# Turning the later contexts and x by 64 rows on both row halves, into the free columns of V's two PSUM banks

## The reference

```python
h = layernorm(x, gamma, beta)                 # x: (8, 256, 256)
Q = (h @ Wq).reshape(B, NQ, 16, 64)           # Wq: 256 x 1024
K = (context @ Wk).reshape(B, NC, 16, 64)     # context: (8, 256, 192)
V = (context @ Wv).reshape(B, NC, 16, 64)
attn = softmax(einsum('bihd,bjhd->bhij', Q, K)) * 64 ** -0.5
vals = einsum('bhij,bjhd->bihd', attn, V).reshape(B, NQ, 1024)
out = x + vals @ Wo + bo
```

## Time and profile before

| What | Value |
|---|---|
| time, median of three runs | 329.81 us |
| time of the profiled execution | 330.24 us |
| its span | 328.2 us |
| PE busy | 320.4 us, 98% of the span |
| DVE busy | 253.5 us, 77% |
| ACT busy | 253.6 us, 77% |
| POOL busy | 155.8 us, 47% |
| mean granted TensorE clock | 0.999 |

### The profile page before, as it was taken

How to read it: one execution, slowest core, us unless ns; L and a number is a source line. 1 busy time by engine, 2 the same in 40 slices (tenths; PEclk the granted TensorE clock), 3 DMA queues, 4 the chain that set the end, 5 groups by cost and what they waited for, 6 DMA issues and landing times.

```text
span 328.2 us, 9691 instructions
## 1 busy us (share of the span) xinstructions
PE 320.4 (98%) x3771; PEld 281.6 (86%) x3771; DVE 253.5 (77%) x591; ACT 253.6 (77%) x798; POOL 155.8 (47%) x288
## 2 busy tenths in 40 slices
PE   5999999999999999999999999999999999999995
PEld 3978888899888889988889988889988888988874
DVE  5798887877778787786878778787777878668784
ACT  4899897877778877888777878787777887776862
POOL 5586578625644256433563336731564425233330
PEclk9999999999999999999999999999999999999999
DMA  6980000020001100020000200002000000000000
GB/s 180 256 257 8 0 2 3 2 91 2 0 3 41 51 3 0 2 90 2 3 3 1 90 2 2 2 1 91 2 2 2 32 3 2 2 3 32 2 3 32
DMA packets 10860, 10.70 MB, mean 33 GB/s; under 512 B 960, under 2 KB 10304, under 8 KB 10816
## 3 DMA queue, kind: packets, MB, share of 16 engines
q1 hardware_dynamic: 10336, 9.77, 10.2%
q10 hardware_dynamic: 416, 0.33, 0.3%
q0 software_dynamic: 64, 0.00, 0.0%
HBM read 8.00 MB, written 2.10 MB: 31 GB/s over the span
## 4 chain that ended last, share of the span: by engine, by line
PE 92%; DVE 3%; ACT 2%; DMA 1%; issue 0%; DVEq 0%
PE mix_ps L919 17%; PE ring_ps L890 14%; PE ring_ps L985 13%; PE o_ps L1025 12%; PE ring_ps L943 11%; PE ring_ps L1062 9%; PE ring_ps L1102 8%; PE ring_ps L1109 3%; ACT prob L469 2%; DMA c_in<-in_ctx_dram 1%; PE ring_ps L963 1%; PE mix_ps L861 1%; PE mix_ps L853 1%; DVE prob_t L830 1%; DVE qk_lo L722 1%; PE mix_ps L1089 0%
## 5 line engine op out<-in xcount | busy, mean ns | idle before, releaser
L378 POOL TENSOR_SCALAR prob<-prob,inv 128x256 f32<-128x256 f32 x192 | 90.3, 487 | 106.5 <-DVE inv L693 106.4
L469 ACT ACTIVATE prob<-ring_ps,neg_max 128x256 f32<-128x256 f32 x256 | 118.4, 476 | 21.6 <-DVE neg_max L686 21.5
L686 DVE TENSOR_REDUCE neg_max<-ring_ps 128x2 f32<-128x512 f32 x128 | 81.4, 678 | 0.4 <-PE ring_ps L890 0.3
L919 PE MATMUL mix_ps<-prob_t,v_sb 128*64 128x256 f32 x496 | 60.6, 386 | 0.3 <-DVE prob_t L830 0.3
L722 DVE TENSOR_TENSOR qk_lo<-ring_ps,qk_hi 128x512 fp32r<-128x512 f32 x64 | 44.2, 691 | 18.2 <-ACT qk_hi L481 18.1
L830 DVE COPY prob_t<-ring_ps 128x512 f32<-128x512 f32 x64 | 41.2, 686 | 21.0 <-PE ring_ps L1062 21.0
L469 ACT ACTIVATION_READ_ACCUMULATOR prob<-ring_ps,neg_max 128x1 f32 x256 | 53.2, 208 | 0.0
L481 ACT ACTIVATE qk_hi<-ring_ps 128x512 fp32r<-128x512 f32 x64 | 38.7, 605 | 13.9 <-PE ring_ps L985 13.9
L919 PEld LDWEIGHTS mix_ps<-prob_t,v_sb 128*64 128x64 f32 x496 | 32.8, 136 | 17.9 <-issue 0.4
L890 PE MATMUL ring_ps<-qk_hi 64*128 64x256 f32 x256 | 39.6, 302 | 0.1
L1062 PE MATMUL ring_ps<-ident,prob 64*128 64x64 f32 x1024 | 37.6, 222 | 0.2 <-DVE prob L712 0.2
(11 more groups left out here) (134 smaller groups left out, 687.4 us busy)
## 6 DMA issues: line engine op xcount, KB each, us to landing
x_in<-in_x_dram SPq DMA_DIRECT2D x8, 256.0 KB, 2.9
out_dram<-y_sb SPq DMA_DIRECT2D x7, 256.0 KB, 2.2
c_in<-in_ctx_dram SPq DMA_DIRECT2D x7, 192.0 KB, 2.9
w_raw<-in_L_xattn_Wq_dram SPq DMA_DIRECT2D x8, 128.0 KB, 3.3
w_raw<-in_L_xattn_Wo_dram SPq DMA_DIRECT2D x4, 256.0 KB, 4.2
w_raw<-in_L_xattn_Wk_dram SPq DMA_DIRECT2D x4, 128.0 KB, 4.1
w_raw<-in_L_xattn_Wk_dram SPq DMA_DIRECT2D x8, 64.0 KB, 3.7
w_raw<-in_L_xattn_Wv_dram SPq DMA_DIRECT2D x2, 256.0 KB, 4.8
```

The costliest lines, as they stand in the source:

```text
L378: last = nc.gpsimd.tensor_scalar(prob[:, e, r, :], prob[:, e, r, :], inv[:, e, r:r + 1], SCALE, ALU.mult, ALU.mult)
L469: last = nc.scalar.activation(prob[:, e, r, :], score_bank(u, e)[:, r * ROWS:(r + 1) * ROWS], ACT.Exp, bias=neg_max[:, e, r:r + 1], accum_ ...
L686: nc.vector.tensor_reduce(neg_max[:, e, :], score_bank(u, e)[:, :].rearrange("p (r j) -> p r j", r=RT), AX, ALU.max, negate=True).then_inc ...
L919: last = nc.tensor.matmul(ps[h * HALF:(h + 1) * HALF, first:first + ROWS], v_sb[:, w // RT % 2, j, p * P + h * HALF:p * P + (h + 1) * HALF ...
```

## The change

The sequences 0 and 1 keep their old transposes. For `b` of 2 to 7 TensorE does `turn_beside` in the same steps as before, but between `values(u + 1)` and `turn(u)`: eight transposes of 64 rows each, alternating between the upper and the lower row half of the array, the upper half's results going to columns 256 to 511 of V's first bank and the lower half's to those of V's second. VectorE copies these columns out to new SBUF tiles (`c_full`, `x_t`), the second bank while ScalarE copies V out of the first, then the first while ScalarE copies V out of the second. ScalarE now starts its copies of V only when `turn_beside` is done. The work that followed reads the SBUF tiles: `context_hi` and `hidden` on ScalarE come after the copies of the probabilities; the low part of the context moves one step later and is split, 128 rows on GpSimd (`context_lo_wide`) and 64 on VectorE (`context_lo_narrow`), followed by GpSimd's `context_for_values`; ScalarE's `context_again` moves two steps later.

```diff
         def context_bank(b):
-            return {0: ring[1][0], 1: o_ps}.get(b, mix_ps)
+            return (ring[1][0], o_ps)[b]
...
+            def context_lo_wide(b):
+                pool.wait_ge(c_hi_ready, b + 1)
+                nc.gpsimd.tensor_tensor(c_t[:, b % 2, 2, :], c_full[:, 0:ROWS],
+                                        c_t[:, b % 2, 0, :].bitcast(fp32), ALU.subtract)\
+                    .then_inc(c_lo_pool_ready, 1)
...
-                b = 1 if u == 2 else of_seq(u, TURN_C, 2)
+                b = 1 if u == 2 else of_seq(u, TURN_X, 2)
                 if b is not None:
+                    if b >= 2:
+                        context_lo_wide(b)
                     context_for_values(b)
...
                     if 2 <= u < STEPS - 1:
                         act.wait_ge(v_made, u + 2)
+                        it = beside(u)
+                        if it is not None:
+                            act.wait_ge(turned_beside, 2 * it[0] + 2)
                         for k, ps in enumerate(qk_banks(u + 1)):
+                            if it is not None and k == 1:
+                                act.wait_ge(beside_out, 2 * it[0] + 1)
                             last = nc.scalar.activation(
                                 v_sb[:, (u + 1) // RT % 2, (u + 1) % RT,
                                      k * V_HALF:(k + 1) * V_HALF],
                                 ps[:, 0:V_HALF], ACT.Copy)
+                            if it is not None and k == 0:
+                                last.then_inc(v_first, 1)
                         last.then_inc(v_ready, 1)
...
+                it = beside(u)
+                if it is not None:
+                    n, b, is_x = it
+                    act.wait_ge(beside_out, 2 * n + 2)
+                    if is_x:
+                        act.wait_ge(h_lo_ready, DT * b)
+                        hidden(b, x_t)
+                    else:
+                        context_hi(b, c_full)
...
+                b = of_seq(u, TURN_X, 2)
+                if b is not None:
+                    context_lo_narrow(b, c_full)
...
-                b = of_seq(u, TURN_C, 2)
-                if b is not None:
-                    context_lo(b, context_bank(b))
+                it = beside(u)
+                if it is not None:
+                    n, b, is_x = it
+                    if is_x:
+                        dve.wait_ge(h_full_ready, DT * b - 1)
+                    elif b >= 3:
+                        context_is_split(dve, b - 1)
+                    dve.wait_ge(turned_beside, 2 * n + 2)
+                    for half in (1, 0):
+                        if half == 0:
+                            dve.wait_ge(v_first, n + 1)
+                        out = (x_t if is_x else c_full)[:, :].rearrange("p (k x i) -> p k x i", x=2, i=HALF)
+                        nc.vector.tensor_copy(out[:, :, half, :],
+                                              qk_banks(u + 1)[half][:, V_HALF:2 * V_HALF]
+                                              .rearrange("p (k i) -> p k i", i=HALF))\
+                            .then_inc(beside_out, 1)
...
+            def turn_beside(u, n, b, is_x):
+                if is_x:
+                    pe.wait_ge(x_norm_ready, b + 1)
+                else:
+                    pe.wait_ge(c_loaded[b % 2], 16 * (b // 2 + 1))
+                for k, (d, r) in enumerate(itertools.product(range(DT), range(RT))):
+                    for half in range(2):
+                        own = slice(half * HALF, (half + 1) * HALF)
+                        if is_x:
+                            rows = x_norm[own, r, d * P:(d + 1) * P]
+                        else:
+                            first = d * (D_CTX - P)
+                            rows = c_in[own, b % 2, r, first:first + P]
+                        first = V_HALF + k * HALF
+                        last = nc.tensor.transpose(qk_banks(u + 1)[half][:, first:first + HALF],
+                                                   rows, ident[own, own])
+                        if k == DT * RT - 1:
+                            last.then_inc(turned_beside, 1)
...
             def scores(u):
                 if u >= 3:
                     pe.wait_ge(v_ready, u + 1)
+                    it = beside(u - 1)
+                    if it is not None:
+                        pe.wait_ge(beside_out, 2 * it[0] + 2)
...
-                b = of_seq(w, TURN_C, 2)
-                if b is not None:
-                    pe.wait_ge(c_lo_ready, b + 1)
-                b = of_seq(w, TURN_X, 1)
-                if b is not None:
-                    pe.wait_ge(h_full_ready, DT * b + 1)
+                if w == 1:
+                    pe.wait_ge(h_full_ready, DT + 1)
...
-                b = of_seq(u, TURN_C, 2)
-                if b is not None:
-                    pe.wait_ge(c_loaded[b % 2], 16 * (b // 2 + 1))
-                    turn_c(b, context_bank(b))
-                b = of_seq(u, TURN_X, 1)
-                if b is not None:
-                    pe.wait_ge(x_norm_ready, b + 1)
+                if u == 1:
+                    pe.wait_ge(x_norm_ready, 2)
                     turn_x((mix_ps, mix_ps), ROWS)
...
                 if 2 <= u < STEPS - 1:
                     values(u + 1)
+                it = beside(u)
+                if it is not None:
+                    turn_beside(u, *it)
                 if u == 0 or 2 <= u < STEPS:
                     turn(u)
```

More of the change, by code:

```diff
@@ L123, in cross_attention_block @@
         inv = sb("inv", [P, HEADS, RT])
+        c_full = sb("c_full", [P, 2 * ROWS])
+        x_t = sb("x_t", [P, DT * ROWS])
         ring = [(bank(f"ring{2 * k}_ps"), bank(f"ring{2 * k + 1}_ps")) for k in range(3)]
@@ L180, in cross_attention_block @@
         c_turned = sem("c_turned")
+        turned_beside = sem("turned_beside")
+        v_first = sem("v_first")
+        beside_out = sem("beside_out")
         h_full_ready = sem("h_full_ready")
@@ L187, in cross_attention_block @@
         c_lo_ready = sem("c_lo_ready")
+        c_lo_pool_ready = sem("c_lo_pool_ready")
         c_rest_ready = sem("c_rest_ready")
@@ L231, in low_ready, with beside, context_is_split, c_is_turned @@
             engine.wait_ge(w_lo_pool_ready, before(n, LO_POOL))
+        def beside(u):
+            for x, offset in enumerate((TURN_C, TURN_X)):
+                b = of_seq(u, offset, 2)
+                if b is not None:
+                    return 2 * (b - 2) + x, b, x == 1
+            return None
+        def context_is_split(engine, b):
+            engine.wait_ge(c_lo_ready, b + 1)
+            if b >= 2:
+                engine.wait_ge(c_lo_pool_ready, b - 1)
+        def c_is_turned(engine, b):
+            if b < 2:
+                engine.wait_ge(c_turned, b + 1)
+            else:
+                engine.wait_ge(turned_beside, 4 * (b - 2) + 2)
+        def x_is_turned(engine, b):
+            if b < 2:
+                engine.wait_ge(x_turned, b + 1)
+            else:
+                engine.wait_ge(turned_beside, 4 * (b - 2) + 4)
         LOAD, STATS, TURN_C, TURN_X, SPLIT_H, PUT = -5, -5, -4, -3, -2, PER_SEQ + 1
@@ L281, in step @@
                     load_x(b)
-                    sp.wait_ge(c_turned, b - 1)
+                    c_is_turned(sp, b - 2)
                     load_c(b)
@@ L326, in norm @@
             def norm(b):
-                pool.wait_ge(x_turned, b)
+                x_is_turned(pool, b - 1)
                 pool.wait_ge(rstd_ready, b + 1)
@@ L339, in context_for_values @@
                     pool.wait_ge(v_made, PER_SEQ * (b - 1))
-                pool.wait_ge(c_lo_ready, b + 1)
+                context_is_split(pool, b)
                 for k in range(CT):
@@ L528, in prepared @@
                 def prepared():
-                    b = of_seq(u, TURN_C, 2)
-                    if b is not None:
-                        act.wait_ge(c_turned, b + 1)
-                        context_hi(b, context_bank(b))
-                    b = of_seq(u, TURN_X, 1)
-                    if b is not None:
-                        act.wait_ge(h_lo_ready, DT * b)
-                        act.wait_ge(x_turned, b + 1)
-                        hidden(b, mix_ps)
+                    if u == 1:
+                        act.wait_ge(h_lo_ready, DT)
+                        act.wait_ge(x_turned, 2)
+                        hidden(1, mix_ps)
                     if u == 2:
@@ L574, in step @@
                     weight_hi(23)
-                b = of_seq(u, TURN_C, 2)
+                it = beside(u)
[7 more added lines that the diff above has]
+                        context_hi(b, c_full)
+                b = of_seq(u, SPLIT_H, 2)
                 if b is not None:
@@ L954, in keys_rest @@
                 if p == 0:
-                    pe.wait_ge(c_lo_ready, b + 1)
+                    context_is_split(pe, b)
                 if p == 0 or u == 1:
```

1 line of the change is left out of this document (removed).

## The result

The changed kernel takes 333.05 us (median of 4 runs, 332.81 to 333.72); the kernel before, run beside it, 329.69 us. The ratio is 1.0101, with its 95% interval from 1.0089 to 1.0114: slower by 1.0%, some 3.4 us. The forecast was slower by 1.7 us, at 331.5, in a range up to 332.9. So the direction came as forecast, and the size was about twice as large.

The account below looks back on a forecast made before the run. TensorE, 98% busy, was taken to bound the kernel. Per step 0.25 added transposes + 0.35 wait - 0.46 removed = +0.14 us, over twelve steps +1.7 on 329.81: 331.5 us, range 329.6 to 332.9.

Parts of the forecast that it names:

- What else moves: Work queued behind the copies on all engines: nothing late relative to the delayed scores, all costed at nothing.
- Eight transposes at 0.25 us: TensorE between values and turn: eight added 64-row transposes, four pairs at 0.062, take 0.25 us per step.
- The removed 0.46: TensorE in twelve steps: dropping the four old transposes and the transition to values saves 0.46 us per step.
- VectorE's copy out of PSUM at 0.41: VectorE's copy of 256 columns from V's bank: 0.41 us, bounds 0.353 and 0.425.
- The release behind transposes: Start of V's bank copies after turn_beside ends: ScalarE 0.07 us behind, VectorE 0.11.
- TensorE's release at 0.23: First scores matmul starts 0.23 us behind VectorE's last copy: 0.14 plus 0.09 for qk_lo_ready; bounds 0.05 and 0.32.
- The wait, 0.35: TensorE ahead of scores: 0.33 us wait for V's banks plus about 0.02 pipeline refill, in each of twelve steps.
- +0.14: Net per step in twelve steps: 0.25 + 0.35 - 0.46 = +0.14 us, together +1.7 us.
- rival 3: Second wait in the same steps, late prob_t copies at a = 1, 0.1 to 0.3 us per step: 333 to 335 us; chance 0.07.
- Rival 2: Cheap handover at scores, low ends hold, gain and wait cancel: 329.7 us, from 329.2 to 330.5; chance 0.17.
- Rival 4: New transposes run singly, not in pairs, 0.25 us more per step: 334.5 us; chance 0.03.
- Rival 1: No wait at scores, evacuation finishes under turn, transposes' gain arrives whole: 327.3 us; chance 0.08.

Follow-up runs that it names:

- Experiment 5: Changed kernel with ScalarE's context_again moved ahead of V's copies in the same step: 330.47 us, ratio 1.002 against the kernel before.
- 11: Kernel of experiment 9 with context_again put back to the end of step 4b - 2: 332.05 us, ratio 1.0072 against the kernel before.
- experiment 6: Kernel before with only context_again moved, from the end of step 4b - 4 to the end of step 4b - 2: 330.69 us, ratio 1.0031.
- experiment 9: Kernel of 8 with satisfied waits moved to the step's head and scores not repeating its qk_lo_ready wait: 329.24 us, ratio 0.998 against the kernel before.
- 10: Control: kernel before without scores' repeated wait for qk_lo_ready: 329.66 us, ratio 0.9994.
- experiment 3: Changed kernel with each engine copying only its own bank, no swap: 332.57 us, ratio 1.0082 against the kernel before.
- 7: Changed kernel with the edits of Experiment 5 and experiment 3 together: 329.95 us, ratio 1.0008 against the kernel before.
- 8: Kernel of 7 with GpSimd's additions into x_bias held until VectorE has scaled in step 4: 330.02 us, ratio 1.0005 against the kernel before.
- 1: Changed kernel with keys_rest's wait for GpSimd's part of the context split moved to ScalarE's context_again: 333.37 us, ratio 1.0107 against the kernel before.
- 2: Kernel before with an always satisfied extra wait added at keys_rest where a sequence begins: 329.78 us, ratio 0.9995.
- 12: Kernel of experiment 6 with ScalarE's copies of V also waiting for turn's first half in twelve steps: 335.98 us, ratio 1.0191 against the kernel before.

## Why the prediction was wrong

**The step that failed is "What else moves", which ended "All of these I cost at nothing".** It went through `prob_t`, `hidden`, the subtractions, GpSimd and SP, and gave no term to a copy that the change also moves: ScalarE's `context_again`, from the end of step 4b - 4 to the end of step 4b - 2. Its reader is `keys_rest`, the next group on TensorE: the copy runs while the scores of step 4b - 1 are being made, and `keys_rest` stands right behind them. Experiment 5 puts it back alone and returns 2.6 us; 11 moves it in another kernel and costs 2.8 us. Ahead of step 7 it ends at T + 2.12 (81.65, with `values` ending at 79.53), and the last scores matmuls start at T + 2.17: no room for the release. That could have been seen from durations in the trace of before. The wait itself is 0.07 us in six steps, 0.4 us; moved alone in the kernel before, the copy cost 1 us (experiment 6). The rest, the slow steps, no row of before would have priced, though its trace had them in steps 29 and 30, right behind the late scores of rows 8, where I read only the 0.33.

Point by point:
- *Eight transposes at 0.25 us*: 0.241. Right. The removed 0.46: 0.456. Right.
- *VectorE's copy out of PSUM at 0.41*: 0.42. Right.
- *The release behind transposes*, 0.07 and 0.11: ScalarE started 0.13, VectorE 0.17 behind T + 0.24. Too low by 0.06.
- *TensorE's release at 0.23*: 0.10 behind VectorE's end, 0.06 behind ScalarE's. Of the 0.09 that I added for `qk_lo_ready` nothing is seen. The Trainium skill, Perfetto Trace Analysis, Identifying Dependency Chains, says that waits on several engines may stand as separate instructions ahead of the waiting one. The trace agrees: three such waits stand ahead of `mix` (experiment 5). Experiments 9 and 10 bound the price at the handover: 0.02 to 0.05 us per step, nothing where none is late.
- *The wait, 0.35*: 0.273. With the lower release the net was +0.058 per step, not +0.14: the handover itself cost 0.7 us and not 1.7. Had nothing else happened, the kernel would stand near 330.5, where experiment 5 is. Of the wait's parts, swapping banks is 0.05 to 0.08 (experiment 3) and the waits in a row 0.02 to 0.05 (experiment 9).
- *No second wait (rival 3)*: the kind was right and the place was wrong. `prob_t` was in time; `c_rest` was late. Its forecast of 333 to 335 us held the result, and that is luck.
- *Rival 2, gain and wait cancel*, is what the kernel is once the stray copy is back in place and each engine keeps its bank (7 and 8).
- *Rival 4*: the transposes took 0.241 and not 0.49, so they ran in pairs.
- *Rival 1*: the gain doesn't arrive whole in any version. The best leaves 1.133 - 0.960 = 0.17 us of wait in each step against a gain of 0.21.
- *Step 4* cost 0.22 us more by GpSimd's additions, which the change starts earlier. I had GpSimd down as 47% busy and so out of the way; it was in VectorE's way.

**What stays open** is what makes a step slow. Seen: it is not the granted clock; in the changed kernel it starts at a late `keys_rest` in five of six cases (and not at that of step 7), and a handover with a wait mostly ends it; it isn't one more semaphore (1, 2), nor the size of the wait (12), nor the late copy alone (6); steps 22 to 24 have it in 7 and 8 without any late copy. Which other condition it takes no run here tells. Only one execution of each kernel was profiled, and the executions of 11 lie 2.7 us apart, so where the slow steps stand, and how many there are, may differ between executions of one kernel. That the 2.6 and 2.8 us are mostly slow steps is therefore shown for 5 against the changed kernel, where the profiled executions differ by as much as the medians, and is not shown for 11.

## What to carry to other kernels

List every instruction that a change moves, the small copies as well, and for each its reader on the bounding engine and the slack left; the one not on the list cost 2.6 us here, the handover that was worked out to the hundredth 0.7 net of the gain. If a kernel is slower without a gap in the chain, compare the same group of matmuls between two steps before looking for new waits. Two banks that two engines emptied went back soonest here where each engine kept its own and the waits that can't be late stood earlier in the step: 0.17 us of wait instead of 0.27.

## What the runs showed of the hardware

- Matmuls with 128 x 128 weights and 256 columns ran at two rates at the same granted clock, one every 113 or every 118 ns (276 or 281 ns each), for whole steps: 0.175 us per step. `mix` (128 x 64 weights, 1.88 us) and `turn` (64 rows, 0.96 us from its start to that of scores where nothing waits) took the same in steps of both kinds.
- Three waits ahead of `mix` whose semaphores were long there passed TensorE's queue 0.11 to 0.13 us apart in step 11. Where they passed under the running scores matmuls one more of them cost nothing (experiment 2); behind a weight load that was 0.05 us late they made `mix` 0.07 us late.
- VectorE's scaling of 128x256 in SBUF took 0.35 us by itself, and two took 1.53 beside GpSimd's additions in SBUF.
- A late copy that costs 0.07 us in each of six steps was worth 2.6 us in one kernel (5), 2.8 in another (11), 1 us in a third (6) and only its own 0.4 in a fourth (12).
